# Opening of the second cross-attention: a wait on GpSimd placed later, two projection pieces per half step of the feed-forward, splits and copies placed earlier, and a smaller fill

## The chip, the cores and the metric

The program runs on one core of a Trainium2 chip. The metric is the device time of one execution in microseconds (us); the time of a kernel is the median of its runs.

## The reference

A state x of 32 batches of 64 tokens by 256 numbers passes through two layers; each has a cross-attention to a context, a self-attention and a feed-forward network, each added to x behind a layer norm. The context is 1601 keys of 256 numbers for every batch.

```python
x = x + L0_xattn(layernorm(x), ctx_1024)     # one head; queries, keys and values projected
x = x + L0_attn(layernorm(x))                # causal, one head of 64
x = x + L0_ffn(layernorm(x))                 # quantised rows, convolution over 3 tokens, silu
x = x + L1_xattn(layernorm(x), ctx_1024)     # 16 heads of 16: kv = ctx @ W_kv, then W_proj, bias
x = x + L1_attn(layernorm(x))                # causal, 16 heads
x = x + L1_ffn(layernorm(x))                 # 2 of 8 experts for each token
return x
```

The part that matters here is the second cross-attention. For each batch, K and V are `ctx @ W_kv` (1601 x 256 each); for each head the scores of 64 queries against 1601 keys go through a softmax and weigh V.

## The kernel before, in words

Every engine has its own program, and the programs meet only in semaphores. The tokens are 16 tiles of 128 (two batches each).

**Stage A** (up to about 404 us) runs over the tiles: cross-attention and self-attention of layer 0, with the layer-0 feed-forward network beside it. The network works in 8 chunks f of 256 tokens and is cut into 47 half steps; `ffn(step)` on each engine issues what falls due in that half step: normalising and quantising (VectorE, `quantise_x`, lines 1647 to 1656), `hidden_group` (TensorE, L1106 and L1107, four groups per chunk), `centre_taps` (ScalarE, L775), `side_taps` (VectorE, L1671 and L1677), `hidden_max` (VectorE, L1683), `hidden_steps` (L1689 to L1697, which end in the diagonal matrices), the row scales (TensorE L1133, copied by ScalarE L788), `scale_hidden` (VectorE, L1703 and L1704) and the second matrix product (TensorE L1139). Chunks overlap by four half steps. After the last tile, half steps 32 to 46 are still to do, and from half step 36 on they are mixed with the projections of the context of batch 0.

**Stage B** is the second cross-attention, with the self-attention and the routing of layer 1 beside it, for 16 pairs of batches. fp32 products are made from rounded halves: `a_hi*b_hi + a_hi*b_lo + a_lo*b_hi`. For the context, SyncE loads one half (`ctx_raw`, one buffer of 801 KB, line 418 or 451), ScalarE rounds it in two parts (`round_ctx`, L850) and GpSimd takes the rest (`split_ctx`, L599); the load of the next half waits for both splits. For one batch the projection has 15 pieces (`PIECES`): 8 K pieces of about 400 keys by 128 features, 6 matmuls each (L1235 to L1237), and 7 V pieces of 256 keys, 12 matmuls each (L1244 to L1246; the last has 6). Two banks of PSUM take turns, so piece p waits for the copies of piece p-2 (`evac` on ScalarE: L837 and L838 for K, L840 and L842 for V). A K piece goes through one of two buffers `k_raw`, which GpSimd has to read (`split_keys`, L591) before ScalarE may fill it for piece p+2.

A batch of stage B is `pe_batch`: TensorE waits for `x_done`, for `k_lo` and the spread queries of this batch, and for the whole context of the next batch (`ctx_lo_ready`); then it makes 16 units of maxima (L1257), each reduced by VectorE (L1803), with the pieces of the next batch among them; the shift is made from the maxima; then come the scores (L1429, L1433), the exponentials (ScalarE L915) and the weighing of V (L1269).

**What lies between A and B before the change.** GpSimd, after its last tile: two splits of batch 0's first context half (L599), the half steps from 33 on, two more splits, a wait for the end of the self-attention (`so_ps`), a memset of all of `vals` (L677, 128 x 7104 numbers; only the column of ones at the end of each 17 is read), the queries split and spread (L610, L604), 8 key splits, four context splits of batch 1, and then a wait for `pads_in` and one for `x_done`, before `pool_pair` of pair 0 (which begins with `spread_queries(1)` and `split_keys(1)`). `pads_in` counts 18 transfers of padding rows to the table `slots_d` in HBM, 1040 KB each (`pad_regions`, L426). The first write that must follow them is the scatter of a routed tile (L627), in pair 2.

SyncE issues one stream in order: context halves as they fall due, and between them 17 small loads of `w_cp4` and the bias (L436, L438), then 6 transfers of padding, load (1,0), 4, load (1,1), 4, load (2,0), 4, load (2,1). Load (n, a) is half a of batch n's context.

ScalarE copies `wkv_hi` (L934) behind half step 33 and rounds the second context half of batch 0 behind half step 34; VectorE makes `wkv_lo` (L1779) behind half step 34. The list `BESIDE_FFN` gives TensorE and ScalarE the order of half steps and pieces: one piece behind each of half steps 36 to 46, then the last four pieces. ScalarE rounds batch 1's context only behind all of that.

Of the kernel before, what the change touches and what calls it, by code (L numbers as in the profile page):

```python
# [19 lines left out]
ALU = mybir.AluOpType  # L20
ACT = mybir.ActivationFunctionType
F32 = mybir.dt.float32
# [55 lines left out]
CTX_AT = {0: (0,), 2: (1,), 8: (2,), 10: (3,)}, {0: (0,), 2: (1,), 6: (2, 3)}  # L78
BESIDE_FFN = list(range(2 * TILES + 4, FFN_STEPS)) + [None] * (len(PIECES) - FFN_STEPS + 2 * TILES + 4)
PROBS = 4  # L80
# [59 lines left out]
def build(nc, io, out):  # L140
    ctx = ExitStack()
    with ctx:
# [254 lines left out]
        def _(sp):  # L397
# [11 lines left out]
            nkeys = ctxN[:, :, :, :].rearrange("p b t n -> p b (t n)")  # L409
            sp.dma_start(nkeys, pair_of(io["ctxN"], 0)).then_inc(s.ctxN_in, 16)  # L410
            with sp.Fori(1, TILES) as i:
                sp.wait_ge(s.scores_ps, i)
                sp.dma_start(ctxT[:, :, :], pair_of(io["ctxT"], i)).then_inc(s.ctxT_in, 16)
                sp.wait_ge(s.av_ps, i)
                sp.dma_start(nkeys, pair_of(io["ctxN"], i)).then_inc(s.ctxN_in, 16)
# [16 lines left out]
            load_ctx(0, 1)  # L432
            sp.wait_ge(s.cp_zero, 6)
            for h in range(HEADS):
                g, j = divmod(h, 4)
                sp.dma_start(w_cp4[32 * j:32 * j + HD, g, :], io["w_cp"][h % HPT * HD:h % HPT * HD + HD, h // HPT, :]).then_inc(s.cp_in, 16)  # L436

            sp.dma_start(w_cp4[HD:HD + 1, 0, :], io["b_p"][0:1, :]).then_inc(s.cp_in, 16)  # L438
            sp.wait_ge(s.ids_ready, 4)
            pad_regions(range(0, 3))  # L440
            load_ctx(1, 0)
            pad_regions(range(3, 5))
            load_ctx(1, 1)
            pad_regions(range(5, 7))
            load_ctx(2, 0)
            pad_regions(range(7, 9))
            load_ctx(2, 1)
            with sp.Fori(3, B) as n:
                for a in range(KT):
# [48 lines left out]
        def _(g):  # L498
# [70 lines left out]
            rsqrt()  # L569
            for i in range(1, TILES + 1):  # L570
                rsqrt(mv_s, rstd_s)
                ffn(2 * i - 1)
                if i < TILES - 1:
                    rsqrt()
            qb = Tally(B=1)
            sqk = Tally(B=3)
# [92 lines left out]
            split_ctx(1)  # L669
            for at in range(2 * TILES + 1, FFN_STEPS):  # L670
                ffn(at)
            rsqrt()
            g.wait_ge(s.av_ps, TILES)
            split_ctx(2)
            split_ctx(3)
            g.wait_ge(s.so_ps, TILES)
            g.memset(vals[:, :, :], 1.0).then_inc(s.ones_ready, 1)  # L677
            split_queries()
            spread_queries(0)
            split_keys(0)  # L680
            for part in range(KT * CTX_PARTS):
                split_ctx(part)
            g.wait_ge(s.pads_in, 16 * SUBS * REGIONS)
            g.wait_ge(s.x_done, XDONE_F)
            pool_pair(True, False, False)
            pool_pair(False, False, False)
            with g.Fori(2, TILES - 1) as i:
                enter("B", i, 2)
                for t in bt:
                    t.enter("B", i, 2)  # L690
                pool_pair(False, False, True)
# [28 lines left out]
        def _(act):  # L720
# [205 lines left out]
            round_ctx(1)  # L926
            copy_xsT()
            copy_qkv()
            ffn(2 * TILES)
            exp_s()  # L930
            copy_pT_s()
            ffn(2 * TILES + 1)
            act.wait_ge(s.wkv_in, 16)
            act.copy(wkv_hi[:, :, :].rearrange("p k n -> p (k n)"), wkv_raw).then_inc(s.wkv_hi_ready, 1)  # L934
            ffn(2 * TILES + 2)
            round_ctx(2)
            round_ctx(3)
            copy_xnT(7)
            ffn(2 * TILES + 3)
            query()  # L940
            T["qbd"].up()
            act.wait_ge(s.ones_ready, 1)
            pieces_evac[0] = 0
            for piece, step in zip(PIECES, BESIDE_FFN):
                if step is not None:
                    ffn(step)
                evac(piece, 0)
            T["k_lo"].up(len(K_PIECES))
# [66 lines left out]
        def _(pe):  # L1015
# [443 lines left out]
            count[0] = 0  # L1459
            for piece, step in zip(PIECES, BESIDE_FFN):  # L1460
                if step is not None:
                    ffn(step)
                if piece == PIECES[0]:
                    pe.wait_ge(s.wkv_lo_ready, 1)
                    pe.wait_ge(s.ctx_lo_ready, T["ctxB"].up(KT * CTX_PARTS))
                project(piece, 0)
            T["k_sb"].up(len(K_PIECES))
# [77 lines left out]
        def _(v):  # L1545
# [221 lines left out]
            for i in range(1, TILES):  # L1767
                vec_pair_a(i)
            norm_s(x[:, TILES - 1, :])
            ffn(2 * TILES - 1)  # L1770
            mask_s()
            ffn(2 * TILES)
# [4 lines left out]
            ffn(2 * TILES + 2)  # L1777
            v.wait_ge(s.wkv_hi_ready, 1)
            v.tensor_tensor(wkv_lo[:, :, :].rearrange("p k n -> p (k n)"), wkv_raw,  # L1779
                            wkv_hi[:, :, :].bitcast(F32).rearrange("p k n -> p (k n)"), ALU.subtract).then_inc(s.wkv_lo_ready, 1)  # L1780
            for step in range(2 * TILES + 3, FFN_STEPS):
# [364 lines left out]
```

## Time and profile before

| | us |
|---|---|
| median of 3 runs | 2762.62 |
| lowest, highest | 2757.52, 2762.82 |
| the profiled execution | 2759.04 |
| its span, first to last instruction | 2757.3 |
| TensorE busy in the span | 2527.0 (92%) |
| VectorE, ScalarE, GpSimd busy | 1699.7, 1377.3, 837.3 |
| mean granted clock of TensorE | 0.964 of 2.4 GHz |

A row of the timeline gives the start and the length in us, the engine, the line and the operation, then what is written and read, how many instructions were merged (xN), and in brackets the idle time before it with what ended it. PE is TensorE, DVE is VectorE, ACT is ScalarE, POOL is GpSimd, and SPq is the queue of SyncE. Rows of the chain of waits give start, length, engine, tile and line. Rows of the table of stretches give the stretch, its length, the busy time of each engine with its number of instructions, the clock granted to TensorE as a share of 2.4 GHz, the busy share of the DMA engines and their GB/s.

### The profile page before, as it was taken

The page shows a single profiled execution, that of the slowest core. Times are in us where ns is not written, and L with a number is a line of the kernel's source. Part 1 is how long each engine was busy: PE and PEld are TensorE (multiplying, and loading weights), DVE is VectorE, ACT ScalarE, POOL GpSimd, SP SyncE. Part 2 cuts the span into 40 slices and gives each one's busy share as a digit, 9 for nine tenths or more (in the row PEclk, how much of TensorE's full clock was granted, in tenths as well). Part 3 has the DMA queues.
Part 4 walks back from the last instruction along what each step waited for, and adds up shares of the span by engine and source line. Part 5 has one row for each costly group of instructions (what it writes and reads, how often), then busy time and mean ns, then how long its engine had stood idle before and what let it go on. Part 6 is the DMA issues. An engine that isn't in the chain of part 4 may idle for free.

```text
span 2757.3 us, 75626 instructions
## 1 busy us (share of the span) xinstructions
PE 2527.0 (92%) x32404; PEld 2173.4 (79%) x32404; DVE 1699.7 (62%) x3035; ACT 1377.3 (50%) x2201; POOL 837.3 (30%) x854
## 2 busy tenths in 40 slices
PE   6999885499999999999999999999999976999997
PEld 3566554388888888888888888888888854999997
DVE  3467778244575575665655755756666555777775
ACT  1233434255555555555555555556555532655653
POOL 1010003234434434344344344343443401111111
PEclk9999997799999999999999999999999976999999
DMA  8876745401101100110011001001100102666664
GB/s 338 313 305 266 285 167 183 148 26 38 38 29 38 42 25 30 42 38 29 30 38 41 30 27 52 26 29 42 38 29 29 64 2 64 224 207 209 208 202 144
DMA packets 61265, 283.47 MB, mean 103 GB/s; under 512 B 5137, under 2 KB 36242, under 8 KB 46354
## 3 DMA queue, kind: packets, MB, share of 16 engines
q1 hardware_dynamic: 52818, 268.73, 26.8%
q0 software_dynamic: 8160, 10.29, 2.3%
q8 instruction: 255, 4.18, 0.6%
q14 instruction: 32, 0.26, 0.0%
HBM read 247.45 MB, written 33.65 MB: 102 GB/s over the span
## 4 chain that ended last, share of the span: by engine, by line
PE 60%; DVE 13%; issue 10%; DMA 6%; POOL 5%; ACT 4%; SPq 1%; DVEq 0%; POOLq 0%; ACTq 0%
PE PS L1433 7%; PE PS L1269 6%; PE PS L1257 5%; DVE mpart L1803 3%; PE PS L1246 3%; PE PS L1244 3%; PE PS L1245 3%; PE PS L1178 3%; PE PS L1429 3%; PE PS L1512 2%; PE PS L1513 2%; POOL ctx_lo L599 2%; PE PS L1514 2%; DMA unit_raw<-in_experts 2%; DVE sideB L1792 2%
## 5 line engine op out<-in xcount | busy, mean ns | idle before, releaser
L1803 DVE TENSOR_REDUCE mpart<-PS 128x1 f32<-128x802 f32 (+1 forms) x512 | 484.9, 986 | 242.5 <-PE PS L1257 241.4
L915 ACT ACTIVATE probs<-PS 128x1024 f32<-128x1024 f32 (+1 forms) x416 | 413.4, 1025 | 214.4 <-PE PS L1433 214.4
L591 POOL TENSOR_TENSOR k_lo<-probs,k_hi 128x400 fp32r<-128x400 f32 (+1 forms) x256 | 250.3, 978 | 286.1 <-ACT k_hi L838 286.1
L599 POOL TENSOR_TENSOR ctx_lo<-ctx_raw,ctx_hi 128x801 fp32r<-128x801 f32 x128 | 223.5, 1757 | 367.6 <-ACT ctx_hi L850 359.0
L1433 PE MATMUL PS<-qbd_hi,k_hi 64*128 64x256 f32 (+1 forms) x1664 | 313.3, 373 | 0.0
L1257 PE MATMUL PS<-k_hi,qbd_hi 128*128 128x512 f32 (+2 forms) x1024 | 266.8, 363 | 29.8 <-POOL ctx_lo L599 15.5
L837 ACT COPY probs<-PS 128x400 f32<-128x400 f32 (+1 forms) x256 | 126.3, 493 | 272.4 <-PE PS L1237 221.1
L1244 PE MATMUL PS<-wkv_hi,ctx_hi 128*128 128x256 f32 (+1 forms) x832 | 236.5, 284 | 0.0
L1433 PE MATMUL PS<-qbd_lo,k_hi 64*128 64x256 f32 (+1 forms) x1664 | 234.3, 278 | 0.0
L1246 PE MATMUL PS<-wkv_hi,ctx_lo 128*128 128x256 f32 (+1 forms) x832 | 234.2, 281 | 0.0
L1433 PE MATMUL PS<-qbd_hi,k_lo 64*128 64x256 f32 (+1 forms) x1664 | 234.1, 278 | 0.0
L1269 PE MATMUL PS<-probs,vals 128*32 128x64 f32 x13312 | 233.3, 221 | 0.6 <-issue 0.5
L1245 PE MATMUL PS<-wkv_lo,ctx_hi 128*128 128x256 f32 (+1 forms) x832 | 233.3, 280 | 0.0
L1269 PEld LDWEIGHTS PS<-probs,vals 128*32 128x32 f32 x13312 | 196.6, 110 | 40.0 <-issue 22.8
L1257 PEld LDWEIGHTS PS<-k_hi,qbd_hi 128*128 128x128 f32 x1024 | 176.6, 193 | 63.8 <-DVE mpart L1803 40.7
L840 ACT COPY vals<-PS 128x512 f32<-128x512 f32 x192 | 112.8, 588 | 220.8 <-PE PS L1246 220.8
L1512 PE MATMUL PS<-xT_hi,unit_hi 128*128 128x256 f32 x736 | 209.5, 285 | 3.2 <-DVE xT_lo L2036 3.0
L1513 PE MATMUL PS<-xT_lo,unit_hi 128*128 128x256 f32 x736 | 208.9, 284 | 0.0
L1514 PE MATMUL PS<-xT_hi,unit_lo 128*128 128x256 f32 x736 | 208.3, 283 | 0.0
L1235 PE MATMUL PS<-ctx_hi,wkv_hi 128*128 128x400 f32 (+1 forms) x512 | 187.8, 367 | 20.2 <-ACT k_hi L838 20.2
L712 POOL DMA_INDIRECT sum_d<-scaled,xg x46 | 75.4, 1640 | 351.7 <-DVE scaled L2067 344.7
L1236 PE MATMUL PS<-ctx_lo,wkv_hi 128*128 128x400 f32 (+1 forms) x512 | 178.5, 349 | 0.0
(318 smaller groups left out, 6259.7 us busy)
## 6 DMA issues: line engine op xcount, KB each, us to landing
unit_raw<-in_experts SPq DMA_DIRECT2D x46, 1536.0 KB, 7.0
ctxN<-in_ctxN SPq DMA_DIRECT2D x16, 3328.0 KB, 11.0
ctxT<-in_ctxT SPq DMA_DIRECT2D x16, 3204.0 KB, 11.2
ctx_raw<-in_ctxT SPq DMA_DIRECT2D x64, 801.0 KB, 4.3
slots_d<-pad_rows SPq DMA_DIRECT2D x18, 1040.0 KB, 12.4
xg<-slots_d SPq DMA_DIRECT2D x23, 260.0 KB, 2.7
x<-in_x SPq DMA_DIRECT2D x1, 2048.0 KB, 10.2
sum_d<-x SPq DMA_DIRECT2D x1, 2048.0 KB, 14.2
```

Source lines behind the costliest of these rows:

```text
L599: g.tensor_tensor(ctx_lo[:, a, cols], ctx_raw[:, cols], ctx_hi[:, a, cols].bitcast(F32), ALU.subtract).then_inc(s.ctx_lo_ready, 1)
L915: act.activation(probs[rows, t % PROBS, :], PS[rows, 1024 * (t % 2):1024 * (t % 2) + 1024], ACT.Exp).then_inc(s.pr_ready, 1)
L1244: pe.matmul(to, ctx_hi[:, k, keys], wkv_hi[:, k, D:2 * D], start=k == 0, stop=False)
L1245: pe.matmul(to, ctx_hi[:, k, keys], wkv_lo[:, k, D:2 * D], start=False, stop=False)
L1246: mm = pe.matmul(to, ctx_lo[:, k, keys], wkv_hi[:, k, D:2 * D], start=False, stop=k == KT - 1)
L1257: mm = pe.matmul(at, qbd_hi[:, n, pair // 4, (pair % 4) * P:(pair % 4) * P + P], k_hi[:, n, pair // 4, c:c + width], start=True, stop=True)
L1269: mm = pe.matmul(bank(4, S, slice(32 * j, 32 * j + 32), g * S), vals[rows, n, mine:mine + 32], probs[rows, t % PROBS, at_head(h):at_head(h ...
L1433: mm = pe.matmul(bank(2 * (t % 2) + r, 256, rows, a * 256), keys_part[part, n, a, keys], queries[part, n, a, r * 256:r * 256 + 256], start ...
L1512: pe.matmul(to, hi[:, k, cols], tokens_hi[:, k, :], start=k == 0, stop=False)
L1513: pe.matmul(to, hi[:, k, cols], tokens_lo[:, k, :], start=False, stop=False)
L1514: mm = pe.matmul(to, lo[:, k, cols], tokens_hi[:, k, :], start=False, stop=k == KT - 1)
L1803: v.tensor_reduce(mpart[:, pair, half:half + 1], PS[:, at:at + width], AX, ALU.max).then_inc(s.mx_red, 1)
```

## The change

GpSimd's wait for `pads_in` stands behind pairs 0 and 1 instead of ahead of pair 0. The loads of `w_cp4` are issued at the very start, behind the first tile's context. Both halves of batch 1's context are loaded before any padding, and the padding is spread over the loads of batches 2 and 3. `BESIDE_FFN` puts two pieces behind each of half steps 36 to 43 (one behind 43) and none behind 44 to 46. The splits of batch 0's context stand ahead of half steps 31 and 33 on GpSimd, and the rounding of its second half ahead of half step 33 on ScalarE. The copy `wkv_hi` and the split `wkv_lo` stand ahead of the last self-attention's scores. Only the column of ones and the tail of `vals` are filled.

```diff
-BESIDE_FFN = list(range(2 * TILES + 4, FFN_STEPS)) + [None] * (len(PIECES) - FFN_STEPS + 2 * TILES + 4)
+BESIDE_FFN = [(2 * TILES + 4 + n, PIECES[2 * n:2 * n + 2]) for n in range(FFN_STEPS - 2 * TILES - 4)]
...
@@ SyncE
             sp.dma_start(nkeys, pair_of(io["ctxN"], 0)).then_inc(s.ctxN_in, 16)
+            sp.wait_ge(s.cp_zero, 6)
+            for h in range(HEADS):
+                g, j = divmod(h, 4)
+                sp.dma_start(w_cp4[32 * j:32 * j + HD, g, :], io["w_cp"][h % HPT * HD:h % HPT * HD + HD, h // HPT, :]).then_inc(s.cp_in, 16)
+
+            sp.dma_start(w_cp4[HD:HD + 1, 0, :], io["b_p"][0:1, :]).then_inc(s.cp_in, 16)
             with sp.Fori(1, TILES) as i:
...
             load_ctx(0, 1)
-            sp.wait_ge(s.cp_zero, 6)
-            for h in range(HEADS):
-                g, j = divmod(h, 4)
-                sp.dma_start(w_cp4[32 * j:32 * j + HD, g, :], io["w_cp"][h % HPT * HD:h % HPT * HD + HD, h // HPT, :]).then_inc(s.cp_in, 16)
-
-            sp.dma_start(w_cp4[HD:HD + 1, 0, :], io["b_p"][0:1, :]).then_inc(s.cp_in, 16)
+            load_ctx(1, 0)
+            load_ctx(1, 1)
             sp.wait_ge(s.ids_ready, 4)
-            pad_regions(range(0, 3))
-            load_ctx(1, 0)
+            pad_regions(range(0, 1))
+            load_ctx(2, 0)
+            pad_regions(range(1, 3))
+            load_ctx(2, 1)
             pad_regions(range(3, 5))
-            load_ctx(1, 1)
+            load_ctx(3, 0)
             pad_regions(range(5, 7))
-            load_ctx(2, 0)
+            load_ctx(3, 1)
             pad_regions(range(7, 9))
-            load_ctx(2, 1)
-            with sp.Fori(3, B) as n:
+            with sp.Fori(4, B) as n:
...
@@ GpSimd
-            for i in range(1, TILES + 1):
+            for i in range(1, TILES):
                 rsqrt(mv_s, rstd_s)
                 ffn(2 * i - 1)
                 if i < TILES - 1:
                     rsqrt()
+            rsqrt(mv_s, rstd_s)
...
             split_ctx(0)
             split_ctx(1)
-            for at in range(2 * TILES + 1, FFN_STEPS):
-                ffn(at)
-            rsqrt()
+            ffn(2 * TILES - 1)
             g.wait_ge(s.av_ps, TILES)
             split_ctx(2)
             split_ctx(3)
+            ffn(2 * TILES + 1)
+            rsqrt()
             g.wait_ge(s.so_ps, TILES)
-            g.memset(vals[:, :, :], 1.0).then_inc(s.ones_ready, 1)
+            for n in range(2):
+                g.memset(vals[:, n, 0:(KEY_TILES - 1) * HEADS * VW].rearrange("p (t d) -> p t d", d=VW)[:, :, HD:VW], 1.0).then_inc(s.ones_ready, 1)
+                g.memset(vals[:, n, (KEY_TILES - 1) * HEADS * VW:], 1.0).then_inc(s.ones_ready, 1)
             split_queries()
             spread_queries(0)
             split_keys(0)
             for part in range(KT * CTX_PARTS):
                 split_ctx(part)
-            g.wait_ge(s.pads_in, 16 * SUBS * REGIONS)
             g.wait_ge(s.x_done, XDONE_F)
             pool_pair(True, False, False)
             pool_pair(False, False, False)
+            g.wait_ge(s.pads_in, 16 * SUBS * REGIONS)
...
@@ ScalarE
             copy_xsT()
+            act.wait_ge(s.wkv_in, 16)
+            act.copy(wkv_hi[:, :, :].rearrange("p k n -> p (k n)"), wkv_raw).then_inc(s.wkv_hi_ready, 1)
             copy_qkv()
             ffn(2 * TILES)
             exp_s()
             copy_pT_s()
-            ffn(2 * TILES + 1)
-            act.wait_ge(s.wkv_in, 16)
-            act.copy(wkv_hi[:, :, :].rearrange("p k n -> p (k n)"), wkv_raw).then_inc(s.wkv_hi_ready, 1)
-            ffn(2 * TILES + 2)
             round_ctx(2)
             round_ctx(3)
+            ffn(2 * TILES + 1)
+            ffn(2 * TILES + 2)
...
-            for piece, step in zip(PIECES, BESIDE_FFN):
-                if step is not None:
-                    ffn(step)
-                evac(piece, 0)
+            for step, beside in BESIDE_FFN:
+                ffn(step)
+                for piece in beside:
+                    evac(piece, 0)
...
@@ TensorE
-            for piece, step in zip(PIECES, BESIDE_FFN):
-                if step is not None:
-                    ffn(step)
-                if piece == PIECES[0]:
-                    pe.wait_ge(s.wkv_lo_ready, 1)
-                    pe.wait_ge(s.ctx_lo_ready, T["ctxB"].up(KT * CTX_PARTS))
-                project(piece, 0)
+            for step, beside in BESIDE_FFN:
+                ffn(step)
+                for piece in beside:
+                    if piece == PIECES[0]:
+                        pe.wait_ge(s.wkv_lo_ready, 1)
+                        pe.wait_ge(s.ctx_lo_ready, T["ctxB"].up(KT * CTX_PARTS))
+                    project(piece, 0)
...
@@ VectorE
             norm_s(x[:, TILES - 1, :])
             ffn(2 * TILES - 1)
+            v.wait_ge(s.wkv_hi_ready, 1)
+            v.tensor_tensor(wkv_lo[:, :, :].rearrange("p k n -> p (k n)"), wkv_raw,
+                            wkv_hi[:, :, :].bitcast(F32).rearrange("p k n -> p (k n)"), ALU.subtract).then_inc(s.wkv_lo_ready, 1)
             mask_s()
...
             ffn(2 * TILES + 2)
-            v.wait_ge(s.wkv_hi_ready, 1)
-            v.tensor_tensor(wkv_lo[:, :, :].rearrange("p k n -> p (k n)"), wkv_raw,
-                            wkv_hi[:, :, :].bitcast(F32).rearrange("p k n -> p (k n)"), ALU.subtract).then_inc(s.wkv_lo_ready, 1)
```

## Rows read from the trace of the kernel before

**Rows 1.** The table of stretches: the last from 565 us to the end.

```profile
565.00:2757.00 2192.00, 2090.91 (x29516) 1870.09 (x29514) 1359.49 (x2226) 1196.56 (x1830) 750.20 (x687) 0.98 0.21 66
```

**Rows 2.** The table of stretches, batch 0 of pair 0.

```profile
501.60:516.10 14.50, 0.00 (x0) 0.00 (x0) 0.00 (x0) 3.13 (x4) 6.87 (x4) 0.60 0.63 183
516.10:525.50 9.40, 9.34 (x36) 8.63 (x36) 4.87 (x5) 1.78 (x4) 0.00 (x0) 0.70 1.09 338
525.50:545.70 20.20, 0.00 (x0) 0.00 (x1) 0.99 (x1) 0.94 (x3) 5.60 (x4) 0.57 0.69 215
545.70:565.30 19.60, 19.59 (x125) 18.49 (x125) 13.08 (x17) 7.88 (x16) 5.80 (x6) 0.92 0.00 1
```

**Rows 3.** The table of waits, 500 to 546 us: who waited for whom, sum, times, longest.

```profile
POOL qbd_hi L604 <- DMA slots_d<-pad_rows: 23.9, 1, 23.9
```

**Rows 4.** The chain of waits, by its start, 501 to 622 us.

```profile
506.15 5.70 DMA ctx_raw<-in_ctxT
...
527.18 12.67 DMA slots_d<-pad_rows
...
621.58 4.24 DMA ctx_raw<-in_ctxT
```

**Rows 5.** The timeline of ScalarE, 487 to 503 us.

```profile
487.51 0.38 ACT L788 COPY rowscale<-PS 128x256 f32<-128x256 f32 x1
...
501.50 1.62 ACT L850 CAST ctx_hi<-ctx_raw 128x801 fp32r<-128x801 f32 x2
```

**Rows 6.** The timeline of VectorE, 409 to 492 us.

```profile
409.20 0.41 DVE L1578 TENSOR_SCALAR xs<-x,mv_s,rstd_s 128x256 f32<-128x256 f32 x1 [0.93 <-POOL rstd_s L553]
...
432.94 1.68 DVE L1578 TENSOR_SCALAR xn<-x,mv,rstd 128x256 f32<-128x256 f32 x1 [1.13 <-POOL rstd L553]
...
438.80 3.38 DVE L1647 TENSOR_SCALAR xf<-x,mv_f,rstd_f 128x256 f32<-128x256 f32 x1
...
443.36 1.77 DVE L1655 TENSOR_SCALAR xf<-xf,small 128x256 f32<-128x256 f32 x1
...
446.96 1.21 DVE L1779 TENSOR_TENSOR wkv_lo<-probs,wkv_hi 128x1024 fp32r<-128x1024 f32 x1
...
487.92 2.29 DVE L1703 TENSOR_TENSOR hidden_f<-hidden_f,rowscale 128x2048 f32<-128x2048 f32 x1 [1.73 <-ACT rowscale L788]
490.24 1.23 DVE L1704 TENSOR_SCALAR hq<-hidden_f 128x2048 bf16<-128x2048 f32 x1
```

**Rows 7.** The timeline of GpSimd, 432 to 473 us.

```profile
432.87 3.21 POOL L599 TENSOR_TENSOR ctx_lo<-ctx_raw,ctx_hi 128x801 fp32r<-128x801 f32 x2
436.02 6.01 POOL L677 MEMSET vals<- 128x7104 f32 x1
...
460.38 1.83 POOL L591 TENSOR_TENSOR k_lo<-probs,k_hi 128x400 fp32r<-128x400 f32 x1 [3.64 <-ACT k_hi L838]
...
472.17 0.90 POOL L591 TENSOR_TENSOR k_lo<-probs,k_hi 128x400 fp32r<-128x400 f32 x1 [2.26 <-ACT k_hi L838]
```

**Rows 8.** The chain of waits, single matmuls of a K piece and a V piece.

```profile
452.67 0.33 PE PS L1235
...
500.95 0.12 PE PS L1245
```

**Rows 9.** The table of stretches, an undisturbed batch from its fifth piece to its scores.

```profile
646.75:664.98 18.23, 18.05 (x127) 17.05 (x126) 14.29 (x19) 7.40 (x15) 4.94 (x5) 1.00 0.00 1
```

**Rows 10.** The timeline of SyncE's queue.

```profile
14.91 3.79 SPq L407 DMA_DIRECT2D w_router<-in_w_router  x1
...
24.08 0.38 SPq L410 DMA_DIRECT2D ctxN<-in_ctxN  x1
...
418.55 7.37 SPq L436 DMA_DIRECT2D w_cp<-in_w_cp  x16
...
518.29 11.85 SPq L426 DMA_DIRECT2D slots_d<-pad_rows  x4
```

**Rows 11.** The timeline of TensorE: the scores of the second tile.

```profile
52.42 5.60 PE L1153 MATMUL PS<-ctxT,qkT 128*64 128x512 f32 x32
```

More of the change, by code:

```diff
@@ L941, in _ @@
             T["qbd"].up()
-            act.wait_ge(s.ones_ready, 1)
+            act.wait_ge(s.ones_ready, 4)
             pieces_evac[0] = 0
-            for piece, step in zip(PIECES, BESIDE_FFN):
-                if step is not None:
-                    ffn(step)
-                evac(piece, 0)
+            for step, beside in BESIDE_FFN:
+                ffn(step)
+                for piece in beside:
+                    evac(piece, 0)
             T["k_lo"].up(len(K_PIECES))
```

## The prediction, on record before the changed kernel ran

> **What bounds the kernel now.** The sum at the end is made against the profiled execution, 2759.0 us (span 2757.3), which lies 3.6 under the median of the runs, 2762.6, and 1.5 over their lowest. I read the table of stretches first, to see where TensorE stands still. From 565 us to the end it is busy for 2091 of 2192 us at a granted clock of 0.98 [rows 1], and nothing that the change edits runs in there except one wait of GpSimd's and some SyncE issues. A time that the start of that stretch gains should therefore reach the end whole. Ahead of it, the same view cut finer shows the opening of batch 0 of pair 0 [rows 2]: 14.5 us in which TensorE does nothing, 9.4 us of work, 20.2 us of nothing again, then 19.6 us of work up to the first scores.
>
> The waits and the chain name the two holes. The second hole is GpSimd's: it sits 23.9 us on the padding transfers [rows 3], of which the last lands 12.67 us after its issue [rows 4]. Behind that wait on its queue stand the key splits; ScalarE may not refill a `k_raw` buffer without them, and TensorE stops ahead of piece 4. The first hole is the context of batch 1: ScalarE rounds it only when all 15 pieces of batch 0 are copied, at 501.5 [rows 5]. Then come two splits, a load of 5.70 us [rows 4], and a second round and split, until 516.1.
>
> **The change, part by part.**
>
> 1. *The wait for the padding, behind pairs 0 and 1.* At the opening GpSimd goes from its last context split straight into the spread and the key splits. The two spreads run while TensorE makes its first maxima and piece, so I expect no stall in the 9.4 us stretch and none behind it: **20.2 us gained** [rows 2]. Its cover is that the scatter comes two pairs later. A group of four transfers takes 11.85 us to issue [rows 10] and 12.67 to land [rows 4]; the last group is issued at the load of context (3,1), inside pair 0, so all is in HBM nearly two batches ahead of the wait. Bounds: 20.2, and 18 if GpSimd, coming out of the splits, is 2 us late for piece 0.
>
> 2. *No second cold start.* After the hole TensorE needed 19.6 us to the scores at a clock of 0.92 [rows 2]; an undisturbed batch needs 18.2 for the same work at 1.00 [rows 9]. **1.3 gained**; bounds 0 and 1.4.
>
> 3. *Two pieces per half step.* The last piece is now behind half step 43, so ScalarE rounds batch 1 right behind the row scales of half step 45, whose copy ends at 487.9 [rows 5], instead of at 501.5: 13.6 us, if the feed-forward chain keeps its time. It does not quite, and three things move it.
>  First, VectorE and GpSimd hold each other up. The memset of `vals` runs from 436.02 to 442.03 [rows 7], and the `tensor_scalar` beside it takes 3.38 us and ends at 442.18, where one of its size takes 0.41 [rows 6]. With the fill cut to some 960 numbers that is 3.0 us back. The next one takes 1.77 [rows 6] beside the spread of the queries, and its twin behind it as long; both are through before the spread once VectorE is on time: 2.8. `xn` takes 1.68 beside a context split that now runs earlier: 1.3. The split `wkv_lo`, 1.21 [rows 6], falls into a wait of VectorE's for the scores. Together 8.3.
>  Second, the same lock elsewhere. The splits moved ahead fall on `xs` (0.41 now, up to 1.6 more, one split being half of 3.21 [rows 6, 7]) and on the quantising of half step 32: I take 2.8 for both. The spread now meets the small steps and the diagonals of half step 35: 2.6. Net so far 2.9 earlier.
>  Third, the extra pieces. A K matmul steps every 0.33 us at the lower clock and a V matmul every 0.12 at the higher one [rows 8], so a K piece is 2.0 us there and a V piece 1.4. The second piece of half step 36 lies in the chain whole (2.0), that of half step 38 about half, and the V pieces behind half step 40 delay the row scales by 1.1; half step 43 gives 0.8 back with its half piece. Sum 3.2. So the chain ends 0.3 later than now. Bounds: 2.9 earlier if VectorE covers all the pieces; 5.0 later if the six pieces that newly stand ahead of the last row scales (five V pieces and a half one, 7.9 us) all lie in it.
>  Rounding then begins 13.3 us earlier. But it now falls beside `scale_hidden`. A key split beside an L1703 took 1.83 us against 0.90 alone [rows 7]: it was held until that instruction, whose inputs both lie in SBUF, had ended. The first context split of batch 1 will be held about 1.4 us by L1703 (2.29), and the second by L1704 (1.23) for half of its length [rows 6]: 2.0 lost; bounds 0 and 2.7. **11.3 gained.** `x_done` comes 2 us later than now at most, still ahead of the context.
>
> 4. *The loads.* Load (1,1) keeps its 5.70 us [rows 4], since two transfers of padding are again issued right behind it; the load at 621.58, with nothing behind it, took 4.24 [rows 4]. I take the first: 0, bounds 0 and 1.5 gained. Here a rule stands against the row. By the Trainium skill, "DMA: Bandwidth & Descriptors", section "Queues, rings and completion order", each DMA engine consumes the descriptors of a queue in ring order, which would let a transfer issued later leave the load alone; by it the sum would be 1.5 better.
>  Loads of batches 2 and 3 now stand behind padding. A group needs 24.5 us from first issue to landing, and such a load is wanted one batch later, behind at least the 9.4 and 18.2 us from maxima to scores [rows 2, 9]; hidden, bounds 0 and 10.5 lost (rival C).
>
> 5. *The early loads.* 17 loads of `w_cp4` and bias stand at 24.5 us, at 0.46 each (16 in 7.37) [rows 10]: SyncE is free at 32.3, and the second tile's context, now issued at 33.1, is used at 52.4 [rows 11]. Nothing. Gone from 418 us, they delayed nobody. `wkv_hi`, and the second context half rounded earlier, fall into idle time of ScalarE: its load is released by GpSimd's splits five us earlier than now and is there. Nothing, bounds 0 and 1.7 (half the two roundings and more) lost.
>
> Sum: 20.2 + 1.3 + 11.3 = **32.8 us**. From 2759.0 that gives 2726.2, from the median of the runs 2729.8; I take 2728.
>
> **The rivals.**
>
> *A. The pieces lie in the feed-forward chain.* For: TensorE is already between VectorE's steps there, often at the lower clock. Against: VectorE, not TensorE, was busy most of the time. Price: 4.7 us to 8 us less, 2731 to 2736. Chance 0.15.
>
> *B. VectorE keeps all it gets back.* For: the four locked instructions are in the chain. Against: each later half step waits for TensorE and ScalarE too. Gain 36 to 38: 2721 to 2724. Chance 0.12.
>
> *C. A context load is late behind padding.* A load behind a group lands at most 24.5 + 4.2 us after the group's first issue [rows 4, 10]; against 18.2 us and more of pieces ahead of its use [rows 9], that is at most 10.5 late, once or twice: 2736 to 2747. Against: a load also has the scores and exponentials of a whole batch ahead of its use. Chance 0.06.
>
> *D. Slower: SyncE is caught at the start.* At 14.9 us one tiny load took 3.79 us to issue with the queue full [rows 10]. If each of the 17 took that, SyncE would be free at 89, the second tile's context would land some 11 us later, 47.7 us after its use at 52.4 [rows 11]: 32.8 - 47.7 gives 2774. It decides from 2.9 us per issue. Against: the big load at 24.08 took 0.38 [rows 10], so the queue has drained. Chance 0.02.
>
> *E. The change doesn't do what it says:* the moved wait stops GpSimd ahead of pair 2 just as long. The padding would have to be out 100 us longer than its 24.5 us groups suggest; gain 12.6, 2746. Chance 0.01.
>
> **How the numbers follow.** The forecast has 0.64. Its own range is 2759.0 - 36 to 2762.8 - 28, or 2723 to 2735. The range given, 2718 to 2739, takes in A and B, the bounds on the lock and the load (0.6 and 1.5 us), and the runs' own spread. This measurement tells about 0.2% (5.5 us) from no change. Faster by over 0.2%: all but D and the worst of C and E, 0.96; within 0.2%: 0.02; slower: 0.02.
>
> **What would show it.** In the profile after: no wait of GpSimd's for `slots_d` in the waits; the first scores of batch 0 near 532 instead of 565; TensorE's first hole from about 492 to 505, and no second one; L1647 at about 0.4 us beside the fill; the first of batch 1's splits stretched beside L1703. A hole of 20 us anywhere in pairs 0 to 2, or a second tile that begins later than 52 us, would make the prediction wrong. If the last row scales come after 491, rival A is right; before 486, B.

## The result, and the profile after

The changed kernel takes 2731.06 us (median of 4 runs, 2724.67 to 2734.65), the kernel before beside it 2760.07 (4 runs, 2757.13 to 2762.82): ratio 0.9894, interval 0.9879 to 0.991, 29 us less. 2728 was forecast, with a range of 2718 to 2739. The profiled execution after took 2731.11, its span is 2729.4; against the span before, 2757.3, that is 27.9 less, and the rest of this text divides these 27.9.

The table of stretches, kernel after:

```profile
486.00:503.20 17.20, 3.72 (x18) 2.26 (x17) 6.10 (x6) 3.51 (x5) 9.32 (x5) 0.60 0.52 153
503.20:532.00 28.80, 28.25 (x189) 26.58 (x189) 18.81 (x23) 12.99 (x25) 11.38 (x10) 0.94 0.64 189
565.00:2729.40 2164.40, 2059.60 (x28872) 1842.75 (x28871) 1354.07 (x2218) 1175.19 (x1801) 739.41 (x680) 0.98 0.22 69
```

Where before there were 9.4 us of work, 20.2 of nothing and 19.6 of work [rows 2], TensorE now works without a break for the whole opening. The waits of the kernel after have none of GpSimd's for `slots_d` up to 700 us. The chain of waits, kernel after, by its start:

```profile
486.54 0.77 ACT ctx_hi L856
487.38 6.04 POOL ctx_lo L603 x2
493.43 5.51 DMA ctx_raw<-in_ctxT
498.97 0.87 ACT ctx_hi L856
499.91 3.17 POOL ctx_lo L603 x2
...
503.21 1.00 PE PS L1263 x2
...
544.24 1.75 issue
...
550.73 2.27 issue
...
590.61 5.22 DMA ctx_raw<-in_ctxT
...
607.41 2.00 issue
```

The upper half is the hole that is left: round, split twice, load, round, split twice. The three "issue" rows are new. They are time in which TensorE stood still with no semaphore to wait for, and no step of the prediction has them.

To see what they cost I mark both kernels at the same places of the program: the end of stage A (the last write of `cat`), the last row scales, the opening of batch 0, the first exponential (it begins with the only table load there) and the copies of the sums at the ends of batches. The timeline of ScalarE, kernel before:

```profile
565.72 1.28 ACT L915 ACT_TABLE_LOAD   x1
587.62 0.37 ACT L897 COPY sums<-PS 128x256 f32<-128x256 f32 x1 [1.76 <-PE PS L1269]
639.67 0.37 ACT L897 COPY sums<-PS 128x256 f32<-128x256 f32 x1 [1.18 <-PE PS L1269]
...
747.31 0.37 ACT L897 COPY sums<-PS 128x256 f32<-128x256 f32 x1 [1.08 <-PE PS L1269]
```

The same, kernel after:

```profile
486.16 0.37 ACT L794 COPY rowscale<-PS 128x256 f32<-128x256 f32 x1 [1.41 <-PE PS L1139]
...
530.01 1.28 ACT L921 ACT_TABLE_LOAD   x1
555.92 0.37 ACT L903 COPY sums<-PS 128x256 f32<-128x256 f32 x1 [4.30 <-PE PS L1275]
612.04 0.37 ACT L903 COPY sums<-PS 128x256 f32<-128x256 f32 x1 [1.18 <-PE PS L1275]
...
719.67 0.37 ACT L903 COPY sums<-PS 128x256 f32<-128x256 f32 x1 [1.09 <-PE PS L1275]
```

The first exponential comes 35.7 us earlier (565.72 to 530.01), the end of batch 0 31.7, the end of batch 1 27.6, the last row (the end of batch 3) 27.6, and the end of the program 27.9. So the opening gained more than was forecast, and 8.1 us were lost again within batches 0 and 1.

One stretch of the program between two marks is a better measure than a total here. The table holds such stretches of the profiled execution of every kernel below. Stage A's end, which none of them edits but by SyncE's early loads, lies between 401.2 and 403.6 us in them, and what follows the fourth sums between 2006.7 and 2013.6: these two, which say nothing of the change, move a total by several microseconds. Each row is one execution. Where the padding is moved away or stands as before, the stretch from first exponential to fourth sums is 181.3 to 181.7; in the four kernels that leave it where the change put it (after, one piece, whole fill, splits late) it is 186.9 to 190.7. So 8.1 is the loss of the one execution after, and 5.3 to 9.1 that of all four.

| kernel | stage A's end to last row scales | to the opening of batch 0 | to the first exponential | to the 4th sums | all four |
|---|---|---|---|---|---|
| before | 83.94 | 28.62 | 49.59 | 181.59 | 343.74 |
| after | 84.11 | 17.05 | 26.80 | 189.66 | 317.62 |
| padding early | 83.14 | 15.88 | 27.75 | 181.62 | 308.39 |
| padding early, again | 83.63 | 15.98 | 27.26 | 181.31 | 308.18 |
| padding twice | 82.82 | 17.07 | 27.19 | 197.25 | 324.33 |
| one in flight | 84.84 | 17.12 | 26.74 | 184.57 | 313.27 |
| wait only | 81.47 | 27.13 | 27.92 | 181.26 | 317.78 |
| one piece | 80.82 | 26.97 | 26.70 | 190.65 | 325.14 |
| whole fill | 88.52 | 16.93 | 27.18 | 187.73 | 320.36 |
| splits late | 83.89 | 17.15 | 26.84 | 186.93 | 314.81 |
| padding early, old splits | 80.34 | 21.38 | 27.87 | 181.74 | 311.33 |
| padding around | 79.65 | 15.80 | 27.66 | 181.71 | 304.82 |

### The profile page after: what moved, and what is told of

Its sections match the earlier page's. It is cut to its first block, busy times and chain, and to the rows that moved or that the text cites. A ratio compares the mean times of both kernels' runs of the same rounds, so it can differ in the third digit from the quotient of the medians.

```text
span 2729.4 us, 75620 instructions
## 1 busy us (share of the span) xinstructions
PE 2522.3 (92%) x32404; PEld 2169.6 (79%) x32404; DVE 1702.9 (62%) x3035; ACT 1377.1 (50%) x2201; POOL 836.4 (31%) x857
## 4 chain that ended last, share of the span: by engine, by line
PE 55%; DVE 13%; issue 13%; DMA 7%; POOL 7%; ACT 4%; SPq 0%; POOLq 0%; DVEq 0%; ACTq 0%
PE PS L1439 7%; PE PS L1275 5%; PE PS L1263 5%; DVE mpart L1809 3%; PE PS L1184 3%; PE PS L1252 3%; PE PS L1250 3%; PE PS L1251 3%; POOL ctx_lo L603 3%; PE PS L1435 3%; DMA unit_raw<-in_experts 3%; DMA sum_d<-scaled,xg 2%; POOL k_lo L595 2%; PE PS L1241 2%; DMA ctx_raw<-in_ctxT 2%
## 6 DMA issues: line engine op xcount, KB each, us to landing
ctxT<-in_ctxT SPq DMA_DIRECT2D x16, 3204.0 KB, 11.3
```

## The three stops

TensorE's timeline, kernel after (in brackets the idle time ahead of the row):

```profile
545.98 0.53 PE L1275 MATMUL PS<-probs,vals 128*32 128x64 f32 x21 [1.75 <-issue]
...
553.00 1.10 PE L1275 MATMUL PS<-probs,vals 128*32 128x64 f32 x63 [2.27 <-issue]
...
609.41 0.28 PE L1439 MATMUL PS<-qbd_lo,k_hi 64*65 64x256 f32 x1 [2.00 <-issue]
```

And the same place of the program as the first of them, kernel before:

```profile
580.23 0.53 PE L1269 MATMUL PS<-probs,vals 128*32 128x64 f32 x21 [0.32 <-issue]
```

In both kernels the first stop falls inside a run of 64 equal matmuls, with 21 still to do. It is a place of the program; only the length differs, 0.32 against 1.75. The table of stretches, kernel after, shows what goes on beside it:

```profile
544.00:546.00 2.00, 0.26 (x18) 0.10 (x7) 0.00 (x0) 1.26 (x2) 0.66 (x1) 1.00 1.07 342
550.70:553.00 2.30, 0.03 (x1) 0.00 (x0) 0.00 (x0) 0.92 (x1) 1.29 (x1) 1.00 1.07 327
```

The clock is at its upper level, and the DMA engines are full at 327 to 342 GB/s: the padding. Beside the third stop, from 607.4 to 609.4 us, it is 387 GB/s. SyncE's queue, kernel after:

```profile
503.49 9.20 SPq L432 DMA_DIRECT2D slots_d<-pad_rows  x4
...
538.99 9.86 SPq L432 DMA_DIRECT2D slots_d<-pad_rows  x4
...
552.41 11.48 SPq L432 DMA_DIRECT2D slots_d<-pad_rows  x4
...
591.01 9.04 SPq L432 DMA_DIRECT2D slots_d<-pad_rows  x4
```

Each stop lies inside or just behind the issuing of such a group, while its transfers still move. Before, the last group was out before the scores [rows 4, 10]. My theory from here on: a transfer of padding in flight delays TensorE's own program, and the padding, now beside scores and weighing, costs the 8.1 us. The rival: the stops belong to the new order of the program or to the execution, and would come without the padding too.

## Experiments on the padding

**Padding early.** All 18 transfers stand between loads (1,0) and (1,1), so that they are through before the opening.

```diff
 load_ctx(1, 0)
-load_ctx(1, 1)
 sp.wait_ge(s.ids_ready, 4)
-pad_regions(range(0, 1))
+pad_regions(range(0, 9))
+load_ctx(1, 1)
 load_ctx(2, 0)
-pad_regions(range(1, 3))
 load_ctx(2, 1)
-pad_regions(range(3, 5))
 load_ctx(3, 0)
-pad_regions(range(5, 7))
 load_ctx(3, 1)
-pad_regions(range(7, 9))
```

> The changed kernel with all 18 padding transfers between loads (1,0) and (1,1), beside the end of the feed-forward chain, and none beside batches 0 and 1. Theory 1 (while the padding moves, TensorE's own program arrives late): the three stops of 1.75, 2.27 and 2.00 us in the scores of pair 0 go back to 0.3 us or nothing, the loads (1,1) and (3,1) land in 4.2 us instead of 5.5 and 5.2, and the kernel gains 7 to 9 us on the changed one (about 2722). It may lose 0 to 4 of them if TensorE is stopped in the feed-forward chain instead. Theory 2 (the stops belong to this piece of TensorE's program, wherever the padding is): the stops stay, and the time is that of the changed kernel within 2 us.

Measured: 2726.24 (2725.22 to 2731.99, 5 runs), ratio 0.9875, interval 0.9856 to 0.9894. No stop of that kind is left, and the stretch from first exponential to fourth sums is 181.62, that of before. By the medians the whole gained 4.8 on the changed kernel, not the 7 to 9 expected, and the intervals of the two ratios overlap: what is shown is the 8.1 in the stretch. SyncE's queue:

```profile
424.38 53.65 SPq L432 DMA_DIRECT2D slots_d<-pad_rows  x18
```

and the chain of waits:

```profile
493.83 4.33 DMA ctx_raw<-in_ctxT
...
585.67 4.55 DMA ctx_raw<-in_ctxT
```

The two loads that carry padding behind them after the change, (1,1) at 5.51 and (3,1) at 5.22, take 4.33 and 4.55 with none. The rival falls: the program of TensorE is the same.

**Padding twice.** Each transfer is also sent to a second table that nobody reads.

```diff
...
+sp.dma_start(spare_by_sub[k, r], pad_rows[:, k, None, :].broadcast_to([P, REGION // SLOT_TILE, ROW])).then_inc(s.pads_in, 16)
...
-g.wait_ge(s.pads_in, 16 * SUBS * REGIONS)
+g.wait_ge(s.pads_in, 32 * SUBS * REGIONS)
```

> The changed kernel with every padding transfer issued twice, the second time to a table that nobody reads, in the same places. Theory 1: each group moves for some 24 us instead of 12 beside pair 0, so stops come at more places or last longer: 5 to 15 us slower than the changed kernel from the first scores of batch 0 to the end of pair 0. Theory 2: the three stops as they are, and at most 2 us for later loads.

Measured: 2741.89 (1 run). The stretch is 7.6 us longer than after the change, 197.25. The chain of waits:

```profile
544.79 2.99 issue
...
554.10 0.70 issue
...
590.92 12.05 DMA ctx_raw<-in_ctxT
...
615.22 1.66 issue
```

With a further 0.93 the stops come to 6.3, against 6.0. They did not double, though the first grew from 1.75 to 2.99: most of what grew is load (3,1), from 5.22 to 12.05, which is 6.8 of the 7.6. In this one run, more padding in the queue prolonged a load that stood behind it and left the sum of the stops nearly as it was.

**One in flight.** SyncE waits for each transfer of padding to land before it issues the next.

```diff
+pads = [0]
...
+pads[0] += 1
+sp.wait_ge(s.pads_in, 16 * pads[0])
```

> The changed kernel, where SyncE waits for each padding transfer to land before it issues the next; the same 18 transfers, groups in the same places, each group spread over some 20 us. Theory 1a (TensorE's program waits behind transfers queued up on the DMA engines): with at most one transfer outstanding the stops of about 2 us shrink to under 1 us each, and the scores of pair 0 are 3 to 6 us shorter than in the changed kernel. Theory 1b (any traffic of the padding's size stops it, however shallow the queue): stops of about 2 us stay, perhaps more of them, since the traffic lasts longer. The loads (3,0) and (4,0) come later, but not late.

Measured: 2727.97 (2727.9 to 2730.76, 4 runs), ratio 0.9879, interval 0.986 to 0.9899. One stop of TensorE is left, at the known place. Its timeline:

```profile
547.66 0.53 PE L1279 MATMUL PS<-probs,vals 128*32 128x64 f32 x21 [1.39 <-issue]
```

The stop is longer than the 1 us expected. The stretch is 5.1 us shorter than after the change, 2.4 to 6.1 shorter than in the four kernels with the padding queued up at these places, and 3.0 longer than without padding. So how much is queued matters, besides that padding moves at all; how much of the loss is due to each, one execution does not say. Load (3,1) still took 5.37.

**The path.** The trace has the transfers that bring the engines their programs: they stand under "instruction" in the table of DMA queues (packets, MB, and the time of the packets as a share of the time of 16 engines). Kernel after, 543 to 554 us:

```profile
q1 hardware_dynamic: 3541, 3.66, 107.1%
q8 instruction: 2, 0.03, 1.2%
```

and with the padding early:

```profile
q1 hardware_dynamic: 122, 0.76, 22.5%
q8 instruction: 2, 0.03, 1.1%
```

Two packets of 16 KB in either, which took about as long, near 1 us each. If one was late, it was late before it moved. That it was late can be read from the single packets of this queue in the traces: the last one that landed before TensorE went on, in us.

| kernel and place of the stop | packet starts | lands | TensorE goes on | behind the landing |
|---|---|---|---|---|
| before, first | 577.98 | 578.92 | 580.23 | 1.31 |
| after, first | 543.69 | 544.62 | 545.98 | 1.36 |
| after, second | 550.35 | 551.46 | 553.00 | 1.54 |
| after, third | 606.74 | 607.94 | 609.41 | 1.47 |
| padding twice, first | 545.17 | 546.29 | 547.79 | 1.50 |
| one in flight, first | 544.86 | 546.15 | 547.66 | 1.51 |

All 19 such stops of TensorE, from 495 to 735 us in the twelve executions, end 1.28 to 1.59 us behind the landing of such a packet. Counted from the first exponential, the packet ahead of the first place starts at 11.3 to 12.3 us in the six executions without padding beside it, at 12.8 with one transfer in flight, at 13.6 to 13.7 after the change, with one piece and with the whole fill, and at 14.8 with the padding twice. With the splits late it starts at 11.6, beside the same padding, and there is no stop at this place. So the stops are taken to be TensorE waiting for its instructions, which 19 cases out of 19 leave little room to doubt, and beside padding their packet mostly starts later. What holds it up before it starts, no run here shows.

## Experiments on the opening

**Wait only.** The kernel before, with nothing but GpSimd's wait moved.

```diff
-g.wait_ge(s.pads_in, 16 * SUBS * REGIONS)
 g.wait_ge(s.x_done, XDONE_F)
...
 pool_pair(False, False, False)
+g.wait_ge(s.pads_in, 16 * SUBS * REGIONS)
```

> The kernel before with GpSimd's wait for the padding moved behind pairs 0 and 1, and nothing else changed. The prediction's steps 1 and 2 give 20.2 + 1.3 = 21.5 us, 2738 to 2739. Theory 1 takes 1 to 4 us of that back, since 8 of the padding transfers still move beside batch 0's maxima and pieces: 2739 to 2743, with stops of TensorE between 516 and 545. Theory 2: the whole 21.5. A rival to both, that something else held TensorE (the next wait in line), would give less than 15.

Measured: 2740.61 (2733.39 to 2742.22, 4 runs), ratio 0.9925, interval 0.9904 to 0.9945: 22.4 under its neighbour's 2763.05, where steps 1 and 2 had 21.5. In the table, opening to first exponential falls by 21.7. The median lies in the range that theory 1 gave, but its stops did not come: there is none, although eight transfers of padding are issued beside its opening, from 501.3 to 524.8 us; TensorE then makes few and long matmuls (maxima and pieces), 36 in 9.4 us [rows 2], where a run of the weighing has 21 in 0.53. The instruction packets fit this: here they start at 517.1 and 536.0, and from then on, beside the scores and the weighing of batch 0, 3.4 to 8.4 us apart. That this is what spares it was not tested by itself.

**One piece.** The kernel after, with one piece behind each half step again.

```diff
-BESIDE_FFN = [(2 * TILES + 4 + n, PIECES[2 * n:2 * n + 2]) for n in range(FFN_STEPS - 2 * TILES - 4)]
+BESIDE_FFN = [(2 * TILES + 4 + n, PIECES[n:n + 1] if n < 10 else PIECES[n:]) for n in range(FFN_STEPS - 2 * TILES - 4)]
```

> The changed kernel with one piece behind each of half steps 36 to 45 and five behind 46, as before. Step 3 of the prediction: the last row scales come 0 to 3 us earlier than in the changed kernel, but ScalarE rounds batch 1's context only at about 498, so batch 0 of pair 0 opens 10 to 13 us later: 2741 to 2744. Rival: the extra pieces had lengthened the feed-forward chain by as much as the early rounding gives, and the time moves by less than 5 us.

Measured: 2741.63 (2739.83 to 2742.8, 4 runs), ratio 0.9924, interval 0.9904 to 0.9945: 0.0030 above the change, some 8 us. The stretches say how: the last row scales come 3.3 us sooner and the opening 9.9 later behind them, 6.6 in the net. So the extra pieces cost the chain about 3, and the early rounding gives back three times that. Stops of 1.96, 0.48 and 2.10 us are at the three places.

**Whole fill.** The kernel after, with `vals` filled in one piece again.

```diff
-for n in range(2):
-    g.memset(vals[:, n, 0:(KEY_TILES - 1) * HEADS * VW].rearrange("p (t d) -> p t d", d=VW)[:, :, HD:VW], 1.0).then_inc(s.ones_ready, 1)
-    g.memset(vals[:, n, (KEY_TILES - 1) * HEADS * VW:], 1.0).then_inc(s.ones_ready, 1)
+g.memset(vals[:, :, :], 1.0).then_inc(s.ones_ready, 4)
```

> The changed kernel with the fill of all 128 x 7104 numbers of vals in one memset again, at its new place on GpSimd. Theory (a memset on GpSimd and a tensor_scalar on VectorE shut each other out): the memset of 6.0 us now begins with VectorE's xn, at about 433; xn takes 6 us instead of 0.7, and the last row scales of the feed-forward come 3 to 6 us later. Rival (VectorE had slack there): xn is long, but the last row scales move by less than 1.5 us, which is as far as this stretch differs between executions of the same code.

Measured: 2737.78 (2733.35 to 2742.34, 4 runs), ratio 0.9918, interval 0.9896 to 0.9941. The last row scales are 4.4 us later than after the change. GpSimd's timeline, with the whole fill:

```profile
434.63 6.02 POOL L681 MEMSET vals<- 128x7104 f32 x1
```

and VectorE's:

```profile
434.72 6.08 DVE L1582 TENSOR_SCALAR xn<-x,mv,rstd 128x256 f32<-128x256 f32 x1 [1.14 <-POOL rstd L556]
```

The `tensor_scalar` began 0.09 us behind the memset and ended 0.15 behind its end; after the change it takes 0.73. Three stops (1.98, 2.01, 1.84) are there as in the kernel after.

**Splits late.** The kernel after, with the context splits, the rounding, `wkv_hi` and `wkv_lo` in their old places (`wkv_lo` on VectorE, moved likewise, isn't shown).

```diff
@@ GpSimd
+ffn(2 * TILES - 1)
 split_ctx(0)
 split_ctx(1)
-ffn(2 * TILES - 1)
+ffn(2 * TILES + 1)
+rsqrt()
...
 split_ctx(3)
-ffn(2 * TILES + 1)
-rsqrt()
@@ ScalarE
-act.wait_ge(s.wkv_in, 16)
-act.copy(wkv_hi[:, :, :].rearrange("p k n -> p (k n)"), wkv_raw).then_inc(s.wkv_hi_ready, 1)
 copy_qkv()
...
-round_ctx(2)
-round_ctx(3)
 ffn(2 * TILES + 1)
+act.wait_ge(s.wkv_in, 16)
+act.copy(wkv_hi[:, :, :].rearrange("p k n -> p (k n)"), wkv_raw).then_inc(s.wkv_hi_ready, 1)
 ffn(2 * TILES + 2)
+round_ctx(2)
+round_ctx(3)
```

> The changed kernel with the splits of batch 0's context, its second rounding, the copy wkv_hi and the split wkv_lo in their old places. By the prediction's terms moving them ahead lost 2.8 us (xs and the quantising of half step 32 shut out) and won 1.3 (xn) and 1.2 (wkv_lo out of the chain): so this comes out 0.3 us faster, nothing that a run can tell. Rival: the part carried some of the gain, and this is 2 us or more slower than the changed kernel, from the end of the stage before to the last row scales.

Measured: 2728.69 (2727.66 to 2730.17, 4 runs), ratio 0.9881, interval 0.9862 to 0.99. The row scales come at 83.89 against 84.11, the opening at 17.15 against 17.05: this part of the change is worth nothing that these traces can tell. `xs` is back at 0.41 us, `xn` at 1.68. Stops of 1.61 and 2.65 us are at the second and third place.

## Looking for a better order

**Padding early, old splits.** The order of the padding of "padding early" and the splits and roundings of "splits late"; `wkv_hi` and `wkv_lo` stay forward.

```diff
 load_ctx(1, 0)
-load_ctx(1, 1)
 sp.wait_ge(s.ids_ready, 4)
-pad_regions(range(0, 1))
+pad_regions(range(0, 9))
+load_ctx(1, 1)
...
@@ ScalarE
-round_ctx(2)
-round_ctx(3)
 ffn(2 * TILES + 1)
 ffn(2 * TILES + 2)
+round_ctx(2)
+round_ctx(3)
...
```

> All padding between loads (1,0) and (1,1) as in the first experiment, and besides the splits and roundings of batch 0's context in their old places, with only wkv_hi and wkv_lo moved forward. Terms: xs back at 0.4 us (1.5 won), the quantising of half step 32 too (1.3 won), xn beside a split again (1.0 lost): 1.8 us better than the first experiment, about 2724. Rival: these waits are covered by TensorE's and ScalarE's, and it equals the first experiment within 1 us.

Measured: 2727.08 (2718.9 to 2729.49, 5 runs), ratio 0.9872, interval 0.9851 to 0.9893. The row scales come at 80.34, 2.8 sooner than with the padding early alone, but the opening is no sooner. The padding was issued 8.7 us later here (433.09) and had not drained. The chain of waits:

```profile
488.82 9.83 DMA ctx_raw<-in_ctxT
```

Load (1,1) took 5.5 us more than the 4.33 above, and used up more than the gain.

**Padding around.** The same, with eight transfers ahead of load (1,0) and ten behind it.

```diff
+sp.wait_ge(s.ids_ready, 4)
+pad_regions(range(0, 4))
 load_ctx(1, 0)
+pad_regions(range(4, 9))
 load_ctx(1, 1)
-sp.wait_ge(s.ids_ready, 4)
-pad_regions(range(0, 1))
...
```

> The seventh experiment with 8 of the 18 padding transfers ahead of load (1,0) and 10 behind it, so that they have landed some 8 us before load (1,1) is issued. In the seventh, load (1,1) stood behind them and took 9.83 us. Theory (queueing behind padding is all that kept the seventh from gaining on the first): load (1,1) takes 4.2 to 4.6 us, from the last row scales to the first maxima of batch 0 it is 16 us as in the first experiment instead of 21, nothing stops in pair 0, and the median is 2720 to 2723. Rival: load (1,0), now behind 8 transfers, is late for batch 1's rounding or TensorE is stopped in the feed-forward chain, and it is no better than 2726.

The kernel of "padding early" was run again beside it, unchanged:

> The first experiment once more, as a measure beside the ninth on the same chip: 2725 to 2727, and 3 to 6 us slower than the ninth if its theory holds, equal within 1 us if its rival does.

Measured: 2725.38 (2717.11 to 2728.1, 4 runs), ratio 0.9872, interval 0.9853 to 0.9892, and 2723.68 (2721.12 to 2728.48, 4 runs), ratio 0.9869, interval 0.9847 to 0.989. The chain of waits, padding around:

```profile
488.37 4.26 DMA ctx_raw<-in_ctxT
```

The load is back at 4.26, and the four stretches together are the shortest of all, 304.82 against 308.18; but the totals do not tell the two apart, and the median is above the 2720 to 2723 expected. The 3.4 us and more lie in the chain to the row scales, where one and the same code gave 83.94 (before) and 81.47 (wait only). I take them as equal. They stand 4.8 to 7.4 us under the changed kernel by their medians, each from its own series and with intervals that overlap the change's; the traces have 7.9 to 8.4 us of it in one stretch, in all four executions whose padding was out early (that with the old splits is the fourth).

## Why the prediction was right, and where it was not

The forecast was right in sign and size, and its 32.8 us stood nearly whole at the first exponential: 35.7 earlier, 1.5 of them from an earlier end of stage A, so 34.2. It came out at 27.9 because 8.1 were lost again and 0.3 gained behind it; the prediction's sum had nothing of that loss. By its steps:

*Steps 1 and 2: right.* 21.5 forecast for opening to first exponential; 22.8 in the trace of the change and 21.7 with only the wait moved. The stretch from 503.2 us ran at 0.94 where the two before had 0.70 and 0.92 [rows 2].

*Step 3: right in sum, its terms only in part.* 11.3 forecast, and 11.4 measured from stage A's end to the opening. The row scales were to come 0.3 later: 0.2. The rounding then began 13.5 sooner (13.3), and rounding to opening is 2.1 longer (2.0). VectorE's timeline, kernel after:

```profile
407.69 1.95 DVE L1584 TENSOR_SCALAR xs<-x,mv_s,rstd_s 128x256 f32<-128x256 f32 x1 [0.93 <-POOL rstd_s L556]
...
433.07 0.73 DVE L1584 TENSOR_SCALAR xn<-x,mv,rstd 128x256 f32<-128x256 f32 x1 [1.14 <-POOL rstd L556]
...
437.96 0.40 DVE L1653 TENSOR_SCALAR xf<-x,mv_f,rstd_f 128x256 f32<-128x256 f32 x1
...
442.32 1.84 DVE L1696 TENSOR_SCALAR small<-small 128x2 f32<-128x2 f32 x1
444.28 1.74 DVE L1699 TENSOR_SCALAR small<-small 128x2 f32<-128x2 f32 x1
...
486.57 2.29 DVE L1709 TENSOR_TENSOR hidden_f<-hidden_f,rowscale 128x2048 f32<-128x2048 f32 x1 [1.21 <-ACT rowscale L794]
488.89 2.78 DVE L1710 TENSOR_SCALAR hq<-hidden_f 128x2048 bf16<-128x2048 f32 x1
```

GpSimd's, kernel after:

```profile
433.26 0.39 POOL L683 MEMSET vals<- 128x288 f32 x1
...
442.24 1.90 POOL L608 TENSOR_TENSOR qbd_hi<-q_hi,head_of 128x1024 fp32r<-128x1024 f32 x1
...
487.38 6.03 POOL L603 TENSOR_TENSOR ctx_lo<-ctx_raw,ctx_hi 128x801 fp32r<-128x801 f32 x2 [15.27 <-ACT ctx_hi L856]
```

Given back: 2.98 at the first `xf` (3.38 to 0.40; 3.0 forecast), 2.9 at the two steps behind it (2.8), 0.95 at `xn` (1.3). Newly met: 1.5 at `xs` and 1.3 at the quantising of half step 32 (2.8 forecast for both), and 3.2 at the two small steps beside the spreads of the queries (1.84 and 1.74 where 0.17 and 0.21 are usual; 2.6 forecast). The first splits of batch 1 took 6.03 where two took 3.21 [rows 7], and L1710 was held in its turn, 2.78 against 1.23 [rows 6]. The extra pieces cost 3.3 (one piece against after), 3.2 forecast (its parts, 2.0, half of that, and 1.1 less 0.8, add up to 3.3). But the same code put the row scales at 83.94 and at 81.47 in two executions: the sum of step 3 agrees more closely than such terms can be known, and that is luck. On the fill, the Trainium skill, "SBUF — State Buffer", section "Who interferes with whom", has VectorE and GpSimd lock each other out of a shared pair of ports for a whole instruction. The whole fill (6.02 beside 6.08) agrees.

*Step 4: right for load (1,1), wrong for the rest, and this is the step that failed.* The load kept 5.51. Of the loads of batches 2 and 3 the prediction said "hidden, bounds 0 and 10.5 lost (rival C)". Load (3,1) was not wholly hidden: 5.22 instead of the 4.24 of [rows 4], 1.0 lost. And the step asked only who waits for a load, not who else draws on the DMA engines. TensorE's stops are 6.0 us, 5.7 more than before (0.3 of such a stop was there). About 1.5 more went to matmuls at the lower clock behind the stop at 550.7: the granted clock was 0.56 from 554.0 to 557.9 us, and from the end of the stop to the second group of maxima it is 4.86 us, where the kernel with the whole fill, at 1.00 in the same place, takes 3.39. Together with the 1.0 of the load that is 8.2, against 8.1 measured. A stop need not bring the lower clock: behind the other two stops of this execution and all three of the whole fill (1.84 to 2.01 us) it stayed at 1.00; with one piece it fell to 0.50 behind the first and the third.

A load took 4.24 to 4.58 us with no padding queued around it (before, padding early twice, padding around, and load (3,1) of wait only and of the old splits), and 5.21 to 5.70 with padding issued right behind it (before, after and six more; with the padding twice, load (3,1) took 12.05). By the ring order of the Trainium skill, "DMA: Bandwidth & Descriptors", section "Queues, rings and completion order", read as the prediction read it, padding issued behind a load would leave it at the first of these. The measurement decides, and the 1.5 us that this would have added were not there.

*Step 5: right.* The 17 early loads took 7.41 us for 16; the second tile's context was issued at 32.25.

*The rivals.* A (row scales after 491) and B (before 486): 486.16, between them, and, with stage A ending where it did before, 487.7, also between them, as forecast. C had the wrong victim. D and E did not happen: stage A's end is 1.5 sooner, and the moved wait no longer shows.

## What to carry to other kernels

A transfer that nobody waits for is not free; here the instruction packets went over the same DMA engines. Put bulk writes where TensorE has few and long instructions, or where it stands still anyway, and not beside runs of short matmuls. Where such a group must stay there, one transfer in flight at a time gave back 5.1 of 8.1 us here (2.4 by the least disturbed of the four kernels), and where it is moved away, see that it has drained before the next load that somebody needs. And when several parts are timed by a total that moves by several microseconds, mark the same places of the program in each trace and compare the stretches.

## What was not expected of the hardware

TensorE stood still for 1.75, 2.27 and 2.00 us beside 327 to 387 GB/s of padding, with no semaphore to wait for, at places of its program where it stands 0.32 us or not at all when no padding moves. It went on 1.28 to 1.59 us after a packet of the instruction queue had landed, in all 19 stops. A `tensor_scalar` of 2 numbers per partition was held 1.6 us by GpSimd's spread of the queries. A load of 801 KB became about 1 us longer by transfers issued behind it, 5.5 longer by a queue ahead of it that had not drained, and 7.8 longer than 4.24 by the doubled padding.
